# State-space loop of a decoder layer: segment sums as two fp32r passes, one of them moved behind the B, x and C projections

## What is computed

```python
z, x, Bm, Cm, dt = split(layernorm(hidden) @ in_proj_w.T)
dt = softplus(dt + dt_bias); A = -exp(A_log)
state = state * exp(dt * A) + dt * outer(x_t, B_t)     # for each token t
y_t = state @ C_t + Dp * x_t
y = y * silu(z); y = y * rsqrt(mean(y*y) + eps) * norm_w
out = y @ out_proj_w.T + mlp + residual                # then a layer norm
```

## Time and profile before

| | before |
|---|---|
| median of 3 runs | 824.4 us (822.17 to 825.23) |
| profiled execution, its own time | 817.42 us |
| span of the profile | 815.7 us |
| busy over the span | PE 721.4 us, DVE 572.6, ACT 457.5, POOL 354.6 |
| mean granted TensorE clock | 0.965 of full |
| segment-sum matmuls (line 901) | 32 records, 592 ns median |
| `tri` on POOL (line 671) | 7, 1.90 us median, 2.35 us longest |

### The profile page before, as it was taken

The page is one execution under the profiler, slowest core; times in us unless marked ns, Lnnn a source line. Parts: engine busy times, 40 slices in busy tenths (PEclk is TensorE's granted clock), DMA queues, the critical chain, the costliest instruction groups (busy, mean ns, idle before and its releaser), DMA issues. The chain is left out here.

```text
span 815.7 us, 15022 instructions
## 1 busy us (share of the span) xinstructions
PE 721.4 (88%) x4930; PEld 643.4 (79%) x4930; DVE 572.6 (70%) x1173; ACT 457.5 (56%) x1002; POOL 354.6 (43%) x513
## 2 busy tenths in 40 slices
PE   4998999556899999999999998688899999999966
PEld 3887676355788888888888887567899999999855
DVE  4864777634778787878787887575477777777436
ACT  4452333235777777777777676233467777777301
POOL 0002666446997777777777774026000000000241
PEclk9999999887999999999999999889999999999978
DMA  9004200060110000000000000326556667662121
GB/s 282 1 1 146 95 1 0 0 226 1 52 34 7 0 6 3 3 6 0 6 0 0 0 1 1 100 66 236 160 170 207 222 223 241 224 210 73 39 78 52
DMA packets 45938, 64.80 MB, mean 79 GB/s; under 512 B 4288, under 2 KB 34880, under 8 KB 45632
## 3 DMA queue, kind: packets, MB, share of 16 engines
q1 hardware_dynamic: 39936, 56.39, 20.8%
q10 hardware_dynamic: 4416, 3.58, 1.6%
q0 software_dynamic: 1536, 4.20, 1.6%
HBM read 53.14 MB, written 11.01 MB: 79 GB/s over the span
## 5 line engine op out<-in xcount | busy, mean ns | idle before, releaser
L1747 POOL DMA_INDIRECT gu_raw<-rows_out,slot x16 | 15.6, 973 | 204.7 <-DMA rows_out<-y_sb 200.1
L1878 ACT ACTIVATE sg<-bg 128x256 f32<-128x256 f32 (+1 forms) x95 | 40.8, 430 | 102.8 <-PE bg L63 94.4
L1203 ACT ACTIVATE prob<-b_s,nb,rs 128x256 f32<-128x256 f32 x128 | 70.9, 561 | 37.5 <-DVE nb L1287 37.1
L61 PE MATMUL bg<-xb_hi,gu_hi 128*128 128x256 f32 x300 | 86.2, 287 | 2.7 <-DVE xb_lo L1991 2.7
L1968 DVE TENSOR_TENSOR hf<-sg,bg 128x256 f32<-128x256 f32 (+1 forms) x95 | 45.0, 474 | 60.0 <-ACT sg L1878 53.8
L1388 POOL TENSOR_SCALAR prob<-prob,rec 128x256 f32<-128x256 f32 x128 | 82.9, 665 | 6.3 <-DVE rec L1333 6.3
L63 PE MATMUL bg<-xb_hi,gu_lo 128*128 128x256 f32 x300 | 84.8, 283 | 0.0
L62 PE MATMUL bg<-xb_lo,gu_hi 128*128 128x256 f32 x300 | 84.8, 283 | 0.0
L61 PE MATMUL bd<-dn_hi,eh_hi 128*128 128x256 f32 x220 | 63.2, 287 | 3.6 <-issue 3.6
L62 PE MATMUL bd<-dn_lo,eh_hi 128*128 128x256 f32 x220 | 63.1, 287 | 3.0 <-issue 3.0
L63 PE MATMUL bd<-dn_hi,eh_lo 128*128 128x256 f32 x220 | 63.5, 288 | 2.4 <-issue 2.4
(11 more groups left out here) (300 smaller groups left out, 2609.5 us busy)
## 6 DMA issues: line engine op xcount, KB each, us to landing
gu_raw<-in_gu SPq DMA_DIRECT2D x17, 1280.0 KB
dn_raw<-in_dn SPq DMA_DIRECT2D x17, 640.0 KB
rows_in<-zero SPq DMA_DIRECT2D x1, 3840.0 KB, 14.0
rows_out<-y_sb SPq DMA_DIRECT2D x30, 128.0 KB, 2.1
x_blk<-rows_in ACTq DMA_DIRECT2D x13, 256.0 KB, 2.7
wq_raw<-in_wq SPq DMA_DIRECT2D x1, 2048.0 KB, 7.8
wkv_raw<-in_wkv SPq DMA_DIRECT2D x1, 2048.0 KB, 12.4
wo_raw<-in_wo SPq DMA_DIRECT2D x4, 512.0 KB, 3.9
```

Source lines behind the costliest of these rows:

```text
L61: pe.matmul(out, lh, rh, start=first, stop=False)
L1203: act.activation(prob[:, g % 2, h, :], b_s[:, h // 2, (h % 2) * MW:(h % 2 + 1) * MW], ACT.Exp, bias=nb[:, h:h + 1], scale=rs[:, g, h:h + 1 ...
L1878: act.activation(sg[:, u % 3, 0:width(u)], gate_of(u), ACT.Silu).then_inc(f_sg, 1)
```

## The change

`dta` is split in the first part into `dta_hi` (cast to fp32r) and `dta_lo` (the remainder), `lower` is cast to fp32r as `lower_r`, and POOL builds two triangular operands, `tri_hi` and `tri_lo`, in place of `tri`. `sums` becomes four fp32r matmuls: for each bank `lower_r` times `tri_hi`, then `lower_r` times `tri_lo`, added in PSUM. In c=1, PE runs `sums` of the next pair behind `project_cbx`, ahead of `b_out`; ACT runs the exponentials of that sequence behind `copies`; POOL runs `norm_scale` and `split_chunk` of c=1 ahead of `mask_decays` and `triangle`.

```diff
@@ first part, POOL and DVE
-                    pool.wait_ge(dta_ready, 1)
-                    pool.tensor_tensor(tri[:, :, :], upper..., dta[:, 0, :]..., ALU.mult).then_inc(tri_ready, 1)
+                    for t, of, ready in ((tri_hi, dta_hi, 2), (tri_lo, dta_lo, 3)):
+                        pool.wait_ge(dta_ready, ready)
+                        pool.tensor_tensor(t[:, :, :], upper..., of[:, 0, :]..., ALU.mult).then_inc(tri_ready, 1)
...
+                        dve.wait_ge(dta_ready, 1)
+                        dve.tensor_copy(dta_hi[:, :, :], dta[:, :, :]).then_inc(dta_ready, 1)
+                        dve.wait_ge(dta_ready, 2)
+                        dve.tensor_tensor(dta_lo[:, :, :], dta[:, :, :], dta_hi[:, :, :].bitcast(F32),
+                                          ALU.subtract).then_inc(dta_ready, 1)
+                        dve.wait_ge(s_const, 16 * 6)
+                        dve.tensor_copy(lower_r[:, :], lower[:, :]).then_inc(lower_ready, 1)
@@ POOL, triangle(n) and step
-                        pool.tensor_tensor(tri[:, :, :], upper..., dta[:, bass.ds(n, 1), :]...
+                        for t, of in ((tri_hi, dta_hi), (tri_lo, dta_lo)):
+                            pool.tensor_tensor(t[:, :, :], upper..., of[:, bass.ds(n, 1), :]...
...
-                        if last and c:
+                        if c:
+                            norm_scale(n - 1, turn_mv)
                             split_chunk(j, c)
                         if not (last and c):
                             mask_decays(n + 1, turn_dec)
                         if not last:
                             triangle(n + 2)
-                        if not (first and c == 0):
+                        if not (first or c):
                             norm_scale(n - 1, turn_mv)
-                        if not (last and c):
+                        if not c:
                             split_chunk(j, c)
@@ ACT, step
-                        if not (last and c):
+                        if not c:
                             decays(n + 1)
...
                             copies(j + 1)
+                            decays(n + 1)
                             gates(j + 1)
@@ PE, sums and step
-                        pe.wait_ge(m_tri, n)
+                        pe.wait_ge(m_tri, n * 2)
...
                         for q in range(2):
-                            mm = pe.matmul(bz[:, q, :], lower[:, :], tri[...], start=True, stop=True)
+                            for t in (tri_hi, tri_lo):
+                                mm = pe.matmul(bz[:, q, :], lower_r[:, :], t[...],
+                                               start=t is tri_hi, stop=t is tri_lo)
...
-                        if c and not last:
-                            sums(n + 1, j * 2 + 2)
...
                             project_cbx(j + 1)
+                            sums(n + 1, j * 2 + 2)
```

More of the change, by code:

```diff
@@ L167, in state_space_layer @@
         lower = sb("lower", [P, P])
-        tri = sb("tri", [P, NH, P])
+        lower_r = sb("lower_r", [P, P], F32R)
+        dta_hi = sb("dta_hi", [P, BATCH, NH], F32R)
+        dta_lo = sb("dta_lo", [P, BATCH, NH], F32R)
+        tri_hi = sb("tri_hi", [P, NH, P], F32R)
+        tri_lo = sb("tri_lo", [P, NH, P], F32R)
         s_wout = sem("s_wout")
@@ L250, in state_space_layer @@
             tri_ready = sem("tri_ready")
+            lower_ready = sem("lower_ready")
             SMALL = 3
@@ L374, in _ @@
                     pool.wait_ge(s_const, 16 * 6)
-                    pool.wait_ge(dta_ready, 1)
-                    pool.tensor_tensor(tri[:, :, :], upper[:, None, :].broadcast_to([P, NH, P]),
-                                       dta[:, 0, :][:, :, None].broadcast_to([P, NH, P]),
-                                       ALU.mult).then_inc(tri_ready, 1)
+                    for t, of, ready in ((tri_hi, dta_hi, 2), (tri_lo, dta_lo, 3)):
+                        pool.wait_ge(dta_ready, ready)
+                        pool.tensor_tensor(t[:, :, :], upper[:, None, :].broadcast_to([P, NH, P]),
+                                           of[:, 0, :].bitcast(F32)[:, :, None].broadcast_to([P, NH, P]),
+                                           ALU.mult).then_inc(tri_ready, 1)
                 @block.vector
@@ L670, in triangle @@
                         pool.wait_ge(m_seg, n)
-                        pool.tensor_tensor(tri[:, :, :], upper[:, None, :].broadcast_to([P, NH, P]),
-                                           dta[:, bass.ds(n, 1), :].rearrange("p b h -> p (b h)")[:, :, None]
-                                           .broadcast_to([P, NH, P]), ALU.mult).then_inc(m_tri, 1)
+                        for t, of in ((tri_hi, dta_hi), (tri_lo, dta_lo)):
+                            pool.tensor_tensor(t[:, :, :], upper[:, None, :].broadcast_to([P, NH, P]),
+                                               of[:, bass.ds(n, 1), :].bitcast(F32).rearrange("p b h -> p (b h)")[:, :, None]
+                                               .broadcast_to([P, NH, P]), ALU.mult).then_inc(m_tri, 1)
                     def mask_decays(n, turn):
@@ L900, in sums @@
                         for q in range(2):
-                            mm = pe.matmul(bz[:, q, :], lower[:, :],
-                                           tri[:, 4 * q:4 * q + 4, :].rearrange("p h l -> p (h l)"),
-                                           start=True, stop=True)
+                            for t in (tri_hi, tri_lo):
+                                mm = pe.matmul(bz[:, q, :], lower_r[:, :],
+                                               t[:, 4 * q:4 * q + 4, :].rearrange("p h l -> p (h l)"),
+                                               start=t is tri_hi, stop=t is tri_lo)
                         mm.then_inc(m_seg, 1)
```

## The result

The kernel with the change takes 829.6 us (median of 6 runs, 824.03 to 831.28), the kernel before, run beside it, 823.5 us (819.78 to 825.62). The ratio is 1.0079, with a 95% interval of 1.0046 to 1.0112: slower by some 6.5 us (the medians are 6.1 apart), where 2.7 were predicted. The time lies in the predicted range (823 to 833 us).

A forecast was written before the change was run, and what follows sets the result against it. PE looked like the bound, but two chains take turns: DVE in c=0, PE in c=1, with DVE standing for POOL. Terms -1.0 + 0.8 + 0 + 4.4 - 1.5 = +2.7 on 824.4 gave 827.1 us; range 823 to 833.

The forecast's parts named there:

- rival D: PE's clock falls in the loop behind the gap ahead of y in c=0: +9 us, 836 us; chance 10%.
- Body pairs: Loop pairs from pair 1 on: POOL's second triangle and order lengthen each from 21.4 to 23.6 us, +4.4 us in all.
- By PE alone 21.2: Body pair if only PE's work counted, with short sums moved behind the projections: 21.2 us instead of 21.4.
- The split ahead of the norm: In c=0 POOL's split issues 0.1 us before DVE's norm, which stands until the split ends; yd at S+10.64.
- rival B: In c=0 the norm gets ahead of POOL's split; a body pair is near 21.8 us, the run 823.5; chance 15%.
- Triangle: Each POOL triangle with fp32r output costs 1.90 us, as the old one; 2.36 kept for the range.
- rival C: A triangle on POOL costs the split's 2.36 us: +5.5, together +8.2, 832.6 us; chance 13%.
- Last pair: Last loop pair, without triangles: short sums and the moved split bring ve to S+14.8; -1.5 us.
- First part: Ahead of the loop: extra DVE casts and subtraction and a second POOL triangle delay wout and the four additions; +0.8 us.
- Ahead of the loop: -1.0: First sums, before pair 0: short fp32r matmuls let PE run on into the projections sooner; -1.0 us.
- Pair 0: 0: First loop pair: no norm waits in c=0, so the next sums come 21.2 us later, as before; 0.
- Rival E: POOL's second triangle hides everywhere and only PE counts: -2.3 to -3.1 us, 821.3 us; chance 7%.

The follow-up runs named there:

- E1: The change with POOL building only one triangle per step, which both passes of the sums read: 821.97 us, ratio 1.0007 to the kernel before.
- E7: The change plus unread matmuls in PE's gaps, with POOL's norm_scale ahead of the triangles and split_chunk behind them: 803.87 us, ratio 0.9979 to the kernel before.
- E9: The change with norm_scale ahead of the triangles and split_chunk behind them on POOL, without unread matmuls: 812.37 us, ratio 1.0064 to the kernel before.
- E6: The change plus unread matmuls in PE's gaps, with POOL's weight split behind ry in c=0: 808.35 us, ratio 1.0043 to the kernel before.
- E4: The change plus unread matmuls, 6 ahead of the loop and 12 behind b_ss in c=0 of every pair: 824.3 us, ratio 1.0027 to the kernel before.
- E2: The change's short sums and two triangles, but sums and all orders placed as in the kernel before: 826.86 us, ratio 1.0072 to the kernel before.
- E5: Short sums and two triangles in the kernel before's orders, plus unread matmuls in PE's gaps: 807.74 us, ratio 0.9996 to the kernel before.

## Why the prediction was right or wrong

The time lies in the range, and in part that is luck. The range was meant to leave rival D out; D's fall of the clock came, and the range held only because it cost 2.9 us and not D's 9. "Within 0.5% of the kernel before", given 0.60, did not come true: 0.79% slower. And a clock of 1.00, a sign of being right, was 0.93 in pairs 0 to 2.

- **Body pairs, right.** Predicted 23.6 us, measured 23.66 and 23.58, and the steps agree. `dec` at S+1.31 (predicted 1.22), mask 2.48 (2.40), split 8.17 (8.13), `yd` 10.68 (10.64), second split 14.88 (14.8), `weights` 18.45 (18.3), triangles' end 22.0 (22.0). E1 and E7 show the cause from both sides: with one triangle, or with another order on POOL, the pair is back at 21.4 to 21.5 where the clock is 1.00. "By PE alone 21.2" was 0.2 too low: E1, E7 and E9 give 21.38 to 21.46, as before the change. So even with POOL and the clock out of the way, the move and the short sums bring a body pair nothing.
- **The split ahead of the norm, right.** Split and norm start 0.24 us apart, the split first, and the norm stands to its end; rival B is out. The rule of the Trainium skill (SBUF — State Buffer, Who interferes with whom), by which of a DVE instruction in a two-port mode and a GpSimd one the first to issue holds the shared pair, agrees with this trace. E6 shows such a wait with `yg`.
- **Triangle, right.** 1.90 us with fp32r output; rival C is out. **Last pair, right:** `ve` at S+14.80 (predicted 14.8), behind the norm that stands for the split.
- **First part, mis-sized.** +0.8 was predicted, +0.3 measured. `wout` took 2.79 us and ran later, and the four additions came in one go behind it. DVE there:

```profile
60.43 1.95 DVE L479 CAST lower_r<-lower 128x128 fp32r<-128x128 f32 x1
62.29 2.79 DVE L508 TENSOR_SCALAR wout<-wout,nw_col 128x256 f32<-128x256 f32 x4
65.01 1.41 DVE L445 TENSOR_TENSOR acc<-bank,x2b 128x256 f32<-128x256 f32 x4
```

  They end 6.6 us behind the start of `dta` (59.79), before 6.35. The additions took the 1.3 us that I had allowed; the term that was off is the end of `wout`, 5.3 us behind `dta` where I had 5.9.
- **"Ahead of the loop: -1.0", wrong: +0.7.** The price of the short sums was right (E4, with the clock at 1.00: 12.00 us, 0.8 less than before), but PE started at the lower level. The change is slower there by 1.5 us than the same instructions at full clock. Before, PE was idle for 1.6 us at this place and kept its clock; after, for 1.89. But E1 and E9 kept it behind 1.89 us and took 12.0: the term holds when the clock does, and whether it does differs between executions of nearly the same instructions.
- **"Pair 0: 0", wrong: +1.6.** Same cause; E4 has 21.50, so 0.3 us of it is not the clock.
- **Rival D, right in its mechanism and given too little.** Its own price, 4.7 us of slow running a pair with 1.6 of slack, was too high: the low stretch takes some 1.4 to 1.5 us of PE's time and just fits into the slack in the body pairs. I worked D out as one case, with the whole price, and took the slack off in all three pairs. I never asked what a shorter fall would cost in the two stretches without slack, where it came to 1.5 and 1.4 us (E4): 2.9 us, beside the 3.8 by which measurement (+6.5) and forecast (+2.7) differ. In the profiled executions the loop and the stretch ahead of it differ from the forecast by just these 2.9 us (5.6 for 2.7); the rest lies outside the loop. The Trainium skill (TensorE: Matmul & The Clock Gate, Why this matters for your kernels) warns of idle gaps between bursts of matmuls, but of longer ones than the 1.9 to 2.1 us here, so it does not by itself make this gap the danger; the traces do, with a fall behind most such gaps. The one row that I set against it, a y at full rate behind such a gap, has no projections behind that y.
- **Rival E, out.** POOL's second triangle does not hide in the change's order. In E7's it does.

What stays open is why the clock falls in one body pair of E1 and E9 and holds in the next, with the same list and a gap of 1.93 us ahead of y in all four, and why it falls in the first stretch of the change and E2 and holds in E1 and E9.

## What to carry to other kernels

When an edit takes matmuls out of a gap or shortens them, look at the granted clock in each stretch that follows, and price a fall separately where another engine's wait covers PE and where none does. A busy share says little about a helper engine: the same 17 us of POOL work cost 2.2 us a pair in one order and nothing in another, because its long instructions stood ahead of the norm and of the mask, which are on the chain. Where two causes overlap in a stretch, removing the covered one alone gives nothing back there, and removing the one that covers it brings the other to light; judge them by stretch and together.

## What the runs showed of the hardware

- PE's granted clock fell to its lower level (spacing 0.21 instead of 0.12 us) behind most idle gaps of 1.9 to 2.3 us (12 of 16 stretches of the change, E1, E2 and E9), and not behind all: E1 and E9 each have gaps of 1.89 and 1.93 us behind which it held. In E6 it fell behind 1.49 us. Behind 12 matmuls that nobody reads, one record of 1.67 us, no y and no projection of E4, E5 and E7 ran slow up to the last pair.
- y itself can run at full rate (1.08 us at 134.89) and the projections right behind it at half: the level changed during or behind it, not in the gap. In the first body pair of E1 it changed some four projections further on.
- Three kinds of DVE operation stood beside a long POOL instruction: the norm, 0.41 to 2.29 us, `yg`, 0.69 to 2.22, and it seems a cast of 128x128, which took 1.95 us beside the first triangle and of which no record stands alone. `sqs` (1.07 us) and `weights` (2.15 us) did not.
